# Row products on GpSimd instead of row dots on VectorE, with every engine's order rewritten

## What is computed

```
v, q, k = relu(x @ Wv + bv), relu(x @ Wq + bq), relu(x @ Wk + bk)
att = softmax(q @ k.T * mask - 9e15 * (1 - mask))      # mask = adj, over 1024 columns
x1  = layernorm(x + relu(att @ v @ Wo + bo))

h = x1 @ W.T + b
u = mask * exp(e[:, None] + f[None, :] + a_b)          # e = h @ a1, f = h @ a2
out = layernorm(x1 + (u / sum(u)) @ h)
```

## Time and profile before

| what | us |
|---|---|
| median of 3 runs (410.75 to 410.81) | 410.78 |
| profiled execution | 413.68 |
| its span, first to last instruction | 411.9 |
| PE busy | 383.0 (93%) |
| VectorE busy | 375.1 (91%) |
| ScalarE busy | 332.7 (81%) |
| GpSimd busy | 264.3 (64%) |

### The profile page before, as it was taken

The page is one execution under the profiler, slowest core; times in us unless marked ns, Lnnn a source line. Parts: engine busy times, 40 slices in busy tenths (PEclk is TensorE's granted clock), DMA queues, the critical chain, the costliest instruction groups (busy, mean ns, idle before and its releaser), DMA issues.

```text
span 411.9 us, 8429 instructions
## 1 busy us (share of the span) xinstructions
PE 383.0 (93%) x2469; PEld 340.8 (83%) x2469; DVE 375.1 (91%) x1245; ACT 332.7 (81%) x660; POOL 264.3 (64%) x249
## 2 busy tenths in 40 slices
PE   7899999999999999899989999899979999898781
PEld 6688987989889988899869889798869989797771
DVE  3997899988899999999899998999898998999886
ACT  5677769997989889797978889798868889888842
POOL 0670856494626987398954988288970995446745
PEclk9999999999999999999999999999999999999795
DMA  5848252478446666289364865477650967486103
GB/s 187 322 149 257 70 211 86 174 267 294 147 186 204 241 228 211 72 277 329 111 250 126 265 228 206 150 241 261 238 180 12 314 252 270 140 305 221 53 1 103
DMA packets 38157, 80.70 MB, mean 196 GB/s; under 512 B 2784, under 2 KB 19680, under 8 KB 38112
## 3 DMA queue, kind: packets, MB, share of 16 engines
q1 hardware_dynamic: 37824, 80.03, 56.1%
q10 hardware_dynamic: 288, 0.14, 0.2%
HBM read 75.96 MB, written 4.19 MB: 195 GB/s over the span
## 4 chain that ended last, share of the span: by engine, by line
PE 55%; DVE 10%; ACT 6%; issue 5%; DMA 4%; POOL 1%; DVEq 1%; SPq 0%; POOLq 0%; ACTq 0%
PE pt_ps L1709 9%; PE av_ps L1721 5%; PE av_ps L1722 5%; PE av_ps L1723 5%; DVE spent L1078 5%; PE m_ps L1742 5%; PE m_ps L1743 4%; PE m_ps L1638 4%; PE s_ps L1631 4%; PE s_ps L1633 4%; PE s_ps L1632 4%; PE m_ps L1639 2%; DMA raw<-in_adj_t_dram 2%; DMA adjt_in<-in_adj_t_dram 1%; ACT adj_t L593 1%
## 5 line engine op out<-in xcount | busy, mean ns | idle before, releaser
L1000 DVE CUSTOM_DVE_ANT_0 prob<-s_ps,penalty 128x1024 f32<-128x1024 f32 x64 | 77.7, 1214 | 12.7 <-PE s_ps L1633 6.8
L1008 DVE TENSOR_TENSOR prob_tl<-pt_ps,prob_th 128x512 fp32r<-128x512 f32 x128 | 85.2, 676 | 3.8 <-ACT prob_th L659 3.7
L651 ACT ACTIVATE prob<-prob,neg_max 128x1024 f32<-128x1024 f32 x64 | 73.8, 1153 | 17.4 <-DVE neg_max L1000 17.0
L401 POOL TENSOR_SCALAR penalty<-raw 128x1024 bf16<-128x1024 f32 x64 | 67.0, 1056 | 31.8 <-issue 21.6
L659 ACT ACTIVATE prob_th<-pt_ps 128x512 fp32r<-128x512 f32 x128 | 74.6, 595 | 14.9 <-PE pt_ps L1709 14.2
L1721 PE MATMUL av_ps<-prob_th,vh 128*128 128x256 f32 x256 | 74.9, 293 | 5.4 <-DVE avl L1013 4.2
L1709 PE MATMUL pt_ps<-ident,prob 128*128 128x128 f32 x512 | 74.6, 276 | 1.9 <-DVE prob_tl L1008 1.7
L1723 PE MATMUL av_ps<-prob_th,vl 128*128 128x256 f32 x256 | 72.3, 283 | 0.0
L1722 PE MATMUL av_ps<-prob_tl,vh 128*128 128x256 f32 x256 | 72.3, 283 | 0.0
L1709 PEld LDWEIGHTS pt_ps<-ident,prob 128*128 128x128 f32 x512 | 58.3, 141 | 10.4 <-DVE prob_tl L1008 3.8
L593 ACT ACTIVATE adj_t<-adjt_in 128x1024 fp32r<-128x1024 f32 x56 | 59.6, 1064 | 2.3 <-DMA adjt_in<-in_adj_t_dram 2.1
(11 more groups left out here) (160 smaller groups left out, 964.3 us busy)
## 6 DMA issues: line engine op xcount, KB each, us to landing
raw<-in_adj_dram SPq DMA_DIRECT2D x64, 512.0 KB, 5.6
adjt_in<-in_adj_t_dram SPq DMA_DIRECT2D x56, 512.0 KB, 3.9
x_in<-in_x_dram SPq DMA_DIRECT2D x8, 512.0 KB, 5.6
raw<-in_adj_t_dram SPq DMA_DIRECT2D x8, 512.0 KB, 5.9
raw<-in_x_t_dram SPq DMA_DIRECT2D x15, 256.0 KB, 3.4
out_dram<-out_sb SPq DMA_DIRECT2D x14, 256.0 KB, 4.3
out_dram<-out_sb SPq DMA_DIRECT2D x4, 128.0 KB, 1.8
wb<-in_pack_b_dram SPq DMA_DIRECT2D x1, 320.0 KB, 3.9
```

The lines of the kernel that those rows point to most:

```text
L401: gp.tensor_scalar(penalty[:, n % RING, :], adj_in[:, n % RING, :], PENALTY, -PENALTY, ALU.mult, ALU.add).then_inc(penalty_done, 1)
L651: sc.activation(prob[i % 2][:, :], prob[i % 2][:, :], ACT.Exp, bias=neg_max[:, i:i + 1], scale=-1.0, accum_out=row_sum[b % 2][:, i:i + 1]) ...
L1000: v.tensor_tensor_reduce(out=prob[i % 2][:, :], in0=s_ps[:, :, :].rearrange("p a n -> p (a n)"), in1=penalty[:, n % RING, :], scale=-1.0, ...
L1008: v.tensor_tensor(prob_tl[n % 2][at], pt_ps[k][:, :].rearrange("p (c n) -> p c n", n=P), prob_th[n % 2][at].bitcast(F32), ALU.subtract).th ...
```

## The change

For batches 0 to 6 the row dots on VectorE are replaced by two steps. dot_weigh(b,k,a) on GpSimd multiplies four normalised tiles (half k) by W a1 or W a2 (a = 0 or 1) into weighed[:, a], one 128x512 instruction, so four a batch. dot_sum(b,k,a) on VectorE adds up each row's 128 products, one tensor_reduce from 512 elements to 4, so four a batch. weighed has one buffer for each a: dot_weigh waits until the half before has been summed. It also waits for all four tiles of norm0's half, where a dot waited for its tile alone. The last batch keeps its dots (now written out in dot_pair). dots_done counts four a batch instead of eight.

```diff
-        spent = sb("spent", [P, 2, 2, D])
+        weighed = sb("weighed", [P, 2, TH, D])
...
+            def dot_weigh(b, k, a):
+                if b == 0 and k == 0 and a == 0:
+                    pool.wait_ge(w1_ok, SET_READ)
+                wait(pool, dots_done, 2 * (2 * b + k) + a - 1)
+                pool.wait_ge(x1_done, T * b + TH * (k + 1))
+                gp.tensor_tensor(weighed[:, a, :, :], x1[b % KEPT][:, tiles(k), :], rows(dot_row[:, a, :], TH),
+                                 ALU.mult).then_inc(weighed_done, 1)
...
-                act.wait_ge(dots_done, T * b + TH * (k + 1))
+                act.wait_ge(dots_done, 2 * (2 * b + k) + 2)
...
-            def dot(b, t):
-                if b == 0 and t == 0:
-                    dve.wait_ge(w1_ok, SET_ALL)
-                wait(dve, ef_done, 2 * (b - 1) + t // TH + 1)
-                dve.wait_ge(x1_done, T * b + t + 1)
-                row_dots(b, t)
-
-            def row_dots(b, t):
-
-                wait(dve, dots_done, T * b + t - 1)
-                stand_alone(dve)
-                for a in range(2):
-                    last = v.tensor_tensor_reduce(out=spent[:, t % 2, a, :], in0=x1[b % KEPT][:, t, :], in1=dot_row[:, a, :], scale=1.0, scalar=0.0,
-                                                  op0=ALU.mult, op1=ALU.add, accum_out=dots[:, t, a:a + 1])
-                last.then_inc(dots_done, 1)
+            def dot_sum(b, k, a):
+                wait(dve, ef_done, 2 * (b - 1) + k + 1)
+                dve.wait_ge(weighed_done, 2 * (2 * b + k) + a + 1)
+                v.tensor_reduce(dots[:, tiles(k), a], weighed[:, a, :, :], AX_X, ALU.add).then_inc(dots_done, 1)
```

Beside this, the slot tables and the lists of calls of all five engines, in head(), batch_pass(p) and tail(), are new. Of the slot tables one line:

```diff
-            ("o", 1, 1, 0), ("o", 1, 2, 1), ("agg", 2, 0, 2), ("k", -1, 0, 0), ("hp", 2, 0, 2), ("o", 1, 3, 1),
+            ("q", -1, 0, 1), ("o", 1, 1, 2), ("agg", 2, 0, 0), ("o", 1, 2, 1), ("agg", 2, 1, 0), ("hp", 2, 0, 2),
```

More of the change, by code:

```diff
@@ L499, in batch_pass @@
             def batch_pass(p):
+                if there(p - 3):
+                    residual1(p - 3, 0)
+                x_lo(p + 1, 0)
                 if there(p - 2):
@@ L538, in tail @@
                 residual1(LAST - 3, 0)
-                residual1(LAST - 3, 1)
-                convert(LAST, 2)
                 g_lo(LAST - 2, 0)
@@ L1172, in dot_pair @@
                 for t in range(2 * j, 2 * j + 2):
-                    row_dots(LAST, t)
+                    dve.wait_ge(dots_done, 4 * LAST + max(t - 1, 0))
+                    stand_alone(dve)
+                    for a in range(2):
+                        last = v.tensor_tensor_reduce(out=weighed[:, a, t % 2, :], in0=x1[LAST % KEPT][:, t, :], in1=dot_row[:, a, :],
+                                                      scale=1.0, scalar=0.0, op0=ALU.mult, op1=ALU.add, accum_out=dots[:, t, a:a + 1])
+                    last.then_inc(dots_done, 1)
             def g_lo_pair(u):
@@ L1357, in batch_pass @@
+                o_bias(p - 1, 2)
+                if there(p - 3):
+                    var_eps1(p - 3)
+                mask_max(p, 2)
+                if there(p - 2):
+                    at_lo(p - 2, 0)
+                prob_lo(p, 0, 1)
                 o_sum(p - 1, 2)
@@ L1504, in tail @@
+                mask_max(LAST, 6)
+                den_out(LAST - 2)
+                inv_den_out(LAST - 2)
+                dot_sum(LAST - 1, 1, 1)
+                scale_out(LAST - 2)
+                prob_lo(LAST, 4, 0)
+                prob_lo(LAST, 4, 1)
                 o_bias(LAST, 0)
-                dot(LAST - 1, 7)
-                hp_out(LAST - 2, 3)
-                prob_lo(LAST, 4, 1)
+                o_sum(LAST, 0)
                 prob_lo(LAST, 5, 0)
-                o_sum(LAST, 0)
@@ L1586, in tail @@
                 inv_den_pair(0)
-                scale_pair(0)
                 at_lo_pair(3)
@@ L1853, in batch_pass @@
                 transpose_p(p - 1, 7, 1)
+                project_q(p + 1, 0)
                 project_out(p - 1, 1)
-                project_out(p - 1, 2)
+                scores(p, 1)
                 if there(p - 2):
@@ L1859, in batch_pass @@
                     aggregate(p - 2, 1)
-                scores(p, 1)
                 transpose_p(p, 0, 0)
-                attend(p - 1, 3)
                 transpose_p(p, 0, 1)
+                project_out(p - 1, 2)
+                scores(p, 2)
                 if there(p - 2):
                     aggregate(p - 2, 2)
+                transpose_p(p, 1, 0)
                 if there(p - 2):
                     aggregate(p - 2, 3)
-                scores(p, 2)
-                project_k(p + 1, 0)
-                transpose_p(p, 1, 0)
+                attend(p - 1, 3)
+                scores(p, 3)
+                if there(p - 2):
+                    aggregate(p - 2, 4)
                 if there(p - 2):
```

807 lines of the change are left out of this document (397 added, 410 removed), and 12 rows, old and new, of tables (HEAD_SLOTS, PASS_SLOTS).

## The result

The changed kernel takes 395.02 us (median of 4 runs, 393.98 to 396.12), the kernel before 410.79. The ratio is 0.959, with an interval of 0.951 to 0.967. The forecast of 401.8 us and its range from 396.5 to 408.5 lie above it; of the rivals the second, 397.0, is the nearest. Three later measurements of it, beside the experiments, gave 0.962, 0.961 and 0.960.

A forecast was written before the change was run, and what follows sets the result against it. PE was taken to bound the passes, with VectorE deciding its idle time. Savings of 3.5, 0.2, 2.8, 0.3, 0.7 and 1.5 us, together 9.0, took 410.78 to 401.8 us; range 396.5 to 408.5.

The forecast's parts named there:

- the gauge: Steady passes against the shorter pass from 87.4 us: 3.7 us less on VectorE takes 1.0 us off a pass.
- the hold-up: Pass from 276.3 to 325.4, where project_k waits 2.5 us for a bank: down to 46.3 us, 2.8 us saved.
- rival 2: More than the sum: PE without gaps from 87.4 to 325.4, 13.8 us saved in all, 397.0 us; chance 0.12.
- PE idle for under 0.5 us a pass: Profile sign in the passes that would show more saved than the forecast's sum.
- the end: From 363.1 us on: batch 5 work moved ahead of the last mask_max and dots no longer late, 1.5 us saved.
- Head stretches: From 14.8 to 87.4 us: PE idle 0.8 and 1.0 us, few dots, 0.3 us saved.
- 325.4 to 363.1: Stretch before the last: half of PE's idle 1.5 us goes, 0.7 us saved.
- Sums: The four new tensor_reduce a batch on VectorE: 0.62 us each, 0.55 to 0.68, without long ones.
- No wait for avl: Sign of a right forecast: PE's attend waits for avl no longer than 0.5 us.
- Rival 4: No change, 410.8 us: GpSimd's longer occupation stops VectorE's other two-operand rows and the sums; chance 0.08.
- Rival 3: Slower, 413.5 us: GpSimd's weighing ends late and, past 2.8 us of room, lengthens every pass; chance 0.13.
- kh without a wait: Sign of GpSimd being late: kh no longer waits for scores, where 1 to 4 us of waiting was forecast.

The follow-up runs named there:

- E14: Changed kernel with adjacency tile 0 queued before tile 1 and four added, unread sums a batch at the normalising of batch p-3: 402.6 us, ratio 0.974.
- E15: Changed kernel with adjacency tile 0 queued before tile 1 and every sum of batches 0 to 6 made twice at its place: 407.4 us, ratio 0.989.
- E3: Kernel before, in its old orders, with the row dots of batches 0 to 6 replaced by one 2-element instruction a tile: 401.21 us, ratio 0.974.
- E13: Changed kernel with adjacency tile 0 queued before tile 1 and two last-batch loads (raw tiles 6 and 3) issued earlier: 393.97 us, ratio 0.953.
- E1: Changed kernel with all new orders, but row dots on VectorE again for batches 0 to 6 and no dot_weigh: 415.4 us, ratio 1.006.
- E10: Kernel before with the split placed by hand in head and passes, plus the changed kernel's tail on all engines: 405.92 us, ratio 0.982.
- E7: Kernel before, in its old orders, with the row dots of batches 0 to 6 replaced by one-input sums over the same rows: 400.04 us, ratio 0.971.
- E2: Kernel before, in its old orders, with dot_weigh and dot_sum put in by hand where the row dots stood: 407.57 us, ratio 0.988.
- E6: Changed kernel with every multiplication of batches 0 to 6 made twice on GpSimd: 428.48 us, ratio 1.040.
- E12: Changed kernel with load_adj_t(p - 1, 0) queued ahead of load_adj_t(p - 1, 1): 394.94 us, ratio 0.957.
- E4: Changed kernel with GpSimd's multiplications left out after the first half of batch 0, the sums reading old values: 398.49 us, ratio 0.967.

## Why the prediction was wrong

**The step that failed** is the gauge: "3.7 us less on VectorE, 1.0 us off the pass", from which "46.5 to 46.3" and "47.5 to 46.3 us, 3.5 us saved" followed. It put the whole 3.7 us down to the normalising of batch p-3 and took a us of it for a us of row dots. E14 and E15 priced the two places in the changed kernel: a us at the normalising's costs a third of a us, at the dots' place a whole one. And the 3.7 us are not all normalising. The shorter pass has as many row dots as the others, but they are held less (a mean of 388 ns against 506 in the pass from 181.3), with GpSimd 10 us less busy beside them:

```profile
87.40:133.90 46.50, 5.42 (x32) 1.00 0.58 205
133.90:181.30 47.40, 6.97 (x32) 1.00 0.62 210
```

With 7.29 and 6.78 us in the next two passes, the row dots make 1.6 us of the difference. If the 2.0 us of normalising were worth 0.1 there, as in the pair of E15, the other 0.9 us go with 1.6 us of row dots. At that price the 4.3 us that the sums save (7.0 to 2.7) give 2.4, a pass of 45.1, and in the shorter pass 2.7 us give 1.5, a pass of 45.0. Both are estimates made after the result, and they come out so near to it also because PE has no wait left there to lose. The passes in fact fell by 2.3 us each, not 1.2, until PE had no wait left: the three steady ones give 6.9 in place of 3.5, the pass from 87.4 gives 1.5 in place of 0.2, the one with the hold-up 3.9 in place of 2.8. That is 5.8 of the 8.5 us by which the sum of 9.0 fell short of 17.5.

**The floor was read wrong too.** I took PE's busy time of 45.6 to 46.1 us as work. E3, E13 and the changed kernel do the same matmuls in 45.3 and 45.0. Part of what a page calls busy was waiting. The rows of matmuls overlap, so a short delay between two need not show as idle time. Transposes and the first matmul of attend in the three steady passes, before and after (busy us, mean ns):

```profile
L1709 PE MATMUL pt_ps<-ident,prob 128*128 128x128 f32 x195 | 28.7, 275 | 0.0
L1721 PE MATMUL av_ps<-prob_th,vh 128*128 128x256 f32 x96 | 28.2, 294 | 3.3 <-DVE avl L1013 3.3
```

```profile
L1711 PE MATMUL pt_ps<-ident,prob 128*128 128x128 f32 x195 | 27.7, 275 | 0.0
L1723 PE MATMUL av_ps<-prob_th,vh 128*128 128x256 f32 x96 | 27.6, 287 | 0.0
```

The same 195 transposes at the same mean cover 1.0 us less, and attend's matmuls, with a median of 283 and 284 ns, 0.6 less: half a us a pass of the 0.9 by which PE's busy time fell. So rival 2, which kept the 230.4 us of busy time over five passes, could not reach the 225.7 us that they last now. Rival 2 comes nearest in the number, and its sign, PE idle for under 0.5 us a pass, is there. But part of that nearness is luck: from 87.4 to 325.4 it had 7.6 us where 12.3 came, and at the end 3.9 where 2.6 came.

**The other terms.** Head stretches 0.3 forecast, 1.4 measured, and 0.2 ahead of them that I had at nothing; "few dots" was a misreading, since the stretch from 49.3 has all sixteen of batch 0, 4.58 us, and gave 1.1 of the 1.4; 325.4 to 363.1 0.7 and 1.0; the end 1.5 and 2.6. E1 has the new tail with the dots at 86.4 us, E3 the old one without them at 85.7, E10 the new one behind old passes at 85.8: no run without all three of relief, new passes and new tail comes to the 82.8 to 83.7 of the changed kernel's four traces. I had named the tail as a place where it could go wrong, and priced it too low.

**What held.** Sums: forecast 0.62 (0.55 to 0.68), measured 0.675 and never above 0.686. By the rule in the Trainium skill's SBUF — State Buffer, section Who interferes with whom, tensor_reduce is not held by GpSimd; the 28 sums here and the 112 of E7 agree. VectorE at 40 to 42 us: 41.2. GpSimd near 40: 39.9. No wait for avl: none. The multiplications take 1.30 us where I took 1.20, which cost nothing in the steady passes, where PE waits for nothing. Rival 4, and the warning of the Trainium skill's Perfetto Trace Analysis, section Optimizing Scalar/DVE Operations, did not come true: E2, the split in old orders, is faster than before, at 0.988 with an interval below 1.

**Rival 3** did not happen, but its room is as good as used up. I had 2.8 us left ahead of kh; 0.2 us of waiting is what the trace shows, and E6 shows each further us of GpSimd coming through at 0.87, though by VectorE, which waits for weighed, and not by kl as rival 3 had it. The sign that I named for it, kh without a wait, was nearly there while the kernel was at its fastest: the loss of a cover shows no price until it is exceeded.

**What the orders did.** Alone nothing (E1). With the relief they turn 45.3 to 46.0 us a pass (E2, E3) into 45.0 and take the tail from 85.7 or more to 82.9. Of the whole ratio, E2 reaches 0.988, or E3 without any row dots 0.974, against about 0.960 of the changed kernel. They also brought a fault of their own, tile 1 queued ahead of tile 0, which E12 and E13 remove. Late adjacency loads as such are not new with them: E7, in the old orders, has a pass of 47.0 us with one.

## What to carry to other kernels

A us of a nearly full engine has a price that depends on its place: before a gauge from two stretches is used, ask whether what differs between them stands where the edit stands; if it doesn't, it is no gauge for the edit. Take the floor of a pass from what the stream of the bounding engine needs without any wait ahead of it, and not from its busy share, which holds some waiting as busy. Where an engine still has instructions with two operands in SBUF, ask of every change on GpSimd what will now stand beside them: E4 left work out and put 0.7 us on VectorE. In a queue of loads, put the one whose buffer comes free first and whose data are needed first ahead; reversed it costs nothing in most passes and up to 1.7 us in one.

## What the hardware showed unexpectedly

A row dot with two operands in SBUF had a median of 284 ns and went up to 1378 (E1), a sum of the same 128x128 tile with one operand 275 and at most 281 (E7), GpSimd being as busy in both (34.95 and 34.96 us a pass). shift, with 8 elements a row, took 0.168 us alone and 0.997 in the median beside a convert (E4). The multiplication of 128x512 on GpSimd took 1.303 us, the addition of the same size in the kernel before 1.202, and another multiplication of that size (L437, whose second operand is one number for each row of a tile) 1.052, so the operation alone does not set the time. ScalarE's wait for the late adjacency load was 3.26 us in one pass of an execution and 1.61 us in the next, with the same program.
